# Mamba and mixture-of-experts layer on one core: shorter routing, the first two units' B spread by TensorE, and the slots of the schedule chosen anew

## What is computed

```python
xn = layernorm(x)
# branch 1 (Mamba): 512 channels, 16 states
x_in, z = split(xn @ W_in)
u = silu(causal_conv4(x_in) + conv_b)
dt, Bm, Cm = split(u @ W_xproj)
delta = softplus(dt @ W_dt + b_dt)
h[t] = exp(delta[t] * A) * h[t-1] + delta[t] * u[t] * Bm[t]      # per channel and state
y[t] = sum_n h[t][n] * Cm[t][n]
out1 = ((y + D_skip * u) * silu(z)) @ W_out
# branch 2 (experts): 16 experts, the best two of each row
probs = softmax(xn @ Wr + br); w, idx = top_k(probs, 2); w /= sum(w)
out2 = sum_k w[k] * (gelu(layernorm(xn @ W1[e] + b1[e])) @ W2[e] + b2[e]),  e = idx[k]
out = x + out1 + out2
```

## Time and profile before

| | |
|---|---|
| median of 3 runs | 1133.63 us (1129.92 to 1133.81) |
| profiled execution | 1137.55 us |
| its span, first to last instruction | 1135.8 us |
| mean granted TensorE clock | 0.902 |

### The profile page before, as it was taken

How to read it: one execution, slowest core, us unless ns; L and a number is a source line. 1 busy time by engine, 2 the same in 40 slices (tenths; PEclk the granted TensorE clock), 3 DMA queues, 4 the chain that set the end, 5 groups by cost and what they waited for, 6 DMA issues and landing times.

```text
span 1135.8 us, 16904 instructions
## 1 busy us (share of the span) xinstructions
PE 940.2 (83%) x4570; PEld 639.2 (56%) x4571; DVE 1045.8 (92%) x1308; ACT 864.9 (76%) x1839; POOL 871.0 (77%) x562
## 2 busy tenths in 40 slices
PE   4927776497998999779998999899988999887865
PEld 3414343363566656556666766576656666666544
DVE  7887999999999988968998989999999999999894
ACT  4544698556698799857999689978998799976971
POOL 5057899699778788756878767977987887887894
PEclk9957887589889999879997999899997999889989
DMA  9576457973376424825447652873457543855313
GB/s 305 188 271 241 137 183 225 316 291 83 112 245 204 107 69 122 312 82 112 103 104 233 210 107 67 255 235 57 107 151 249 133 116 87 291 169 108 70 19 65
DMA packets 119367, 185.86 MB, mean 164 GB/s; under 512 B 12012, under 2 KB 104344, under 8 KB 111016
## 3 DMA queue, kind: packets, MB, share of 16 engines
q1 hardware_dynamic: 87120, 144.60, 37.7%
q0 software_dynamic: 19584, 25.26, 13.0%
q10 hardware_dynamic: 12568, 14.93, 4.3%
HBM read 146.34 MB, written 42.60 MB: 166 GB/s over the span
## 4 chain that ended last, share of the span: by engine, by line
PE 36%; DVE 18%; issue 16%; ACT 14%; POOL 9%; DMA 4%; ACTq 2%; SPq 1%; POOLq 0%; DVEq 0%
DVE hb L1555 10%; PE psY L1087 8%; POOL hc L624 5%; PE psA L1112 4%; PE psC L1225 4%; PE psA L1160 3%; ACT hb L798 3%; PE psE L1202 3%; PE psC L1175 3%; PE psA L1104 2%; DVE psB L1544 2%; ACT hnT L913 2%; PE psA L1148 2%; DMA xg<-xs_d 1%; POOL xs_d L638 1%
## 5 line engine op out<-in xcount | busy, mean ns | idle before, releaser
L624 POOL TENSOR_TENSOR hc<-hb,Cb 128x1024 f32<-128x1024 f32 x245 | 621.2, 2640 | 108.2 <-PE psY L1087 65.4
L1555 DVE TENSOR_TENSOR_SCAN hb<-hb,carry,psB 128x512 f32<-128x512 f32 x384 | 470.9, 1261 | 6.8 <-ACT hb L798 5.0
L798 ACT ACTIVATE hb<-delta,aneg 128x512 f32<-128x512 f32 x512 | 351.9, 716 | 27.5 <-POOL hc L624 21.0
L1087 PE MATMUL psY<-ident,hc 128*128 128x128 f32 x2048 | 308.0, 292 | 71.1 <-POOL hc L624 70.8
L1087 PEld LDWEIGHTS psY<-ident,hc 128*128 128x128 f32 x2048 | 258.1, 151 | 183.8 <-POOL hc L624 94.1
L1544 DVE TENSOR_TENSOR psB<-Bb,psU 128x512 f32<-128x512 f32 x512 | 324.6, 678 | 3.2 <-DMA Bb<-bc_d 3.2
L672 POOL DMA_INDIRECT out<-yo,idx x80 | 128.8, 1610 | 56.8 <-DMA out<-yo,idx 16.9
L1555 DVE TENSOR_TENSOR_SCAN hb<-hb,psB 128x512 f32<-128x512 f32 x128 | 149.3, 1202 | 0.0
L1112 PE MATMUL psA<-ux,dgw 128*128 128x512 f32 x232 | 114.0, 607 | 1.6 <-ACT ux L739 1.4
L1225 PE MATMUL psC<-w2r,hnT 128*128 128x256 f32 x320 | 89.8, 429 | 0.0
L631 POOL TENSOR_TENSOR du<-delta,ux 128x512 f32<-128x512 f32 x32 | 47.2, 1474 | 53.9 <-DVE delta L1377 51.8
(11 more groups left out here) (233 smaller groups left out, 1198.2 us busy)
## 6 DMA issues: line engine op xcount, KB each, us to landing
Bb<-bc_d SPq DMA_DIRECT2D x32, 1024.0 KB, 7.1
Cb<-bc_d SPq DMA_DIRECT2D x32, 1024.0 KB, 7.4
w1r<-w1c_d SPq DMA_DIRECT2D x80, 256.0 KB
w2r<-in_L_ffn_W SPq DMA_DIRECT2D x80, 256.0 KB, 3.4
xg<-xs_d SPq DMA_DIRECT2D x20, 516.0 KB
xg<-xn_d SPq DMA_DIRECT2D x37, 128.0 KB, 2.8
Bb<-in_L_attn_x SPq DMA_DIRECT2D x8, 512.0 KB, 8.2
xn_d<-hb SPq DMA_DIRECT2D x8, 512.0 KB, 7.9
```

Source lines behind the costliest of these rows:

```text
L624: pool.tensor_tensor(hc[:, k:k + 2, :], hb[:, g % HR:g % HR + 2, :], Cb[:, n:n + 2, :], ALU.mult).then_inc(s_g, 1)
L798: act.activation(hb[:, g % HR, :], delta[:, dc, :], ACT.Exp, scale=aneg[:, dc, n:n + 1]).then_inc(s_exp, 1)
L1087: mm = pe.matmul(y[:, tt * P:(tt + 1) * P], hc[:, g % GR, tt * P:(tt + 1) * P], ident[:, :], start=False, stop=(n == NS - 1), is_transpose ...
L1555: dve.tensor_tensor_scan(h, h, psB[g % 2][:, :], first, ALU.mult, ALU.add).then_inc(s_scan, 1)
```

## The change

- *Norm tiles*: the last of the four tiles of each group is normalised by GpSimd (`norm_tile`), between its convolution weights. Readers wait for both counters; the statistics of a group wait until the tile two groups earlier is done.
- *Routing*: the one-hot selections run in two halves of 256 elements, each as soon as its half of the logits is copied. The second weight comes from exp(second logit - first), a 128 x 32 activation on ScalarE, and not from a masked sum. The rank matmul uses -1/0 weights (`later`) and a layout by experts, so that the copy, a subtraction, the comparison and its sum go; tiles per expert come from rounding count / 128. VectorE computes the slots ahead of the list of empty rows; GpSimd copies them to integers.
- *First units*: the rows of B of units 0 and 1 are spread by two TensorE matmuls (`b_all`) straight into the PSUM banks of the products; VectorE makes the first du, ScalarE copies it to PSUM behind the second exponential. SyncE loads the second quarter of B and C ahead of the rows. Eight of the 16 zero tiles are written in units 0 to 7 and not ahead of them.
- *Tables*: many slots of `AT`, `AT0`, `AT7` and `MOE` move; `HC_DVE` loses 204, 274 and 416 and gains 14 and 64; the additions of the last chunk come two slots earlier.

```diff
-INIT_AT = 58
-ETAB_AT = 40
+INIT_AT = 57
+ETAB_AT = 38
...
+BP = 2
...
 AT = {
-    "x_load": [36],
+    "x_load": [34],
...
-    "xd_mm": [39, 41, 41, 44],
+    "xd_mm": [41, 41, 42, 43],
...
-    "d_max": [55, 58, 62, 4],
-    "du": [53, 0, 25, 26],
+    "d_max": [55, 59, 63, 5],
+    "du": [53, 0, 23, 26],
...
 AT0 = {
...
-    "d_mm": [46, 50, 59, 6],
...
-    "d0_exp": [4, 6, 6],
-    "d0_max": [7, 8, 8],
-    "du": [50, 8, 21, 35],
...
+    "d_mm": [49, 51, 60, 1],
...
+    "d0_exp": [3, 6, 7],
+    "d0_max": [3, 4, 7],
+    "du": [50, 7, 20, 32],
...
 AT7 = {
...
-    "p_tr": [53, 56, 59, 61],
-    "p_trc": [56, 58, 59, 62],
-    "p_mm": [56, 58, 59, 61],
-    "p_copy": [58, 58, 61, 62],
+    "p_tr": [48, 56, 57, 58],
+    "p_trc": [56, 57, 58, 59],
+    "p_mm": [56, 57, 59, 60],
+    "p_copy": [57, 58, 59, 60],
 }
 
-HC_DVE = [2, 10, 12, 20, 54, 56, 86, 180, 204, 274, 416]
+HC_DVE = [2, 10, 12, 14, 20, 54, 56, 64, 86, 180]
...
+ZERO0 = 8
+ZERO_STEP = 1
...
 MOE = {
-    "load": [0],
-    "load1": [0, 3],
-    "load2": [12],
+    "load": [1],
+    "load1": [1, 3],
+    "load2": [13],
...
-    "idx": [6],
+    "idx": [4],
...
+def zero_unit(k):
+
+    return (k - ZERO0) * ZERO_STEP
...
+        def norm_tile(eng, g, tt):
+
+            eng.wait_ge(s_rs, g + 1)
...
             load_bc(0, 0)
+            load_bc(0, 1)
             sp.wait_ge(s_w["bst"], 16 * 6)
             sp.wait_ge(s_route, 1)
             for j in range(NPLACE):
                 load_rows(j)
-            for q in range(1, NS // NQ):
+            for q in range(2, NS // NQ):
                 load_bc(0, q)
...
             pool.wait_ge(s_w["conv"], 32)
-            for dc in range(DC):
-                conv_weights(dc)
+            for g in range(NC):
+                norm_tile(pool, g, TT - 1)
+                if g >= 1 and g - 1 < 2 * DC - 2:
+                    conv_weights((g - 1) // 2, (g - 1) % 2)
+            for h in range(2):
+                conv_weights(DC - 1, h)
...
-            du_mul(0, 0)
+
+            pool.wait_ge(s_slots, 1)
+            pool.tensor_copy(slots[:, :, :], small[:, 5:7, :]).then_inc(s_route, 1)
             for k in range(NPAD):
-                put_zeros(k)
+                if zero_unit(k) < 0:
+                    put_zeros(k)
...
+                if g == 1:
+                    act.wait_ge(s_du0, 1)
+                    act.activation(psU[:, :], du[:, :], ACT.Copy).then_inc(s_dup, 1)
...
-            act.wait_ge(s_rtd, 1)
+            act.wait_ge(s_rtd, 3)
             act.activation(scratch[7], scratch[6], ACT.Exp).then_inc(s_rte, 1)
+            act.wait_ge(s_rtd, 5)
+            act.activation(small[:, 6, :], small[:, 7, :], ACT.Exp).then_inc(s_rte, 1)
...
+            def b_all(n):
+
+                if n == 0:
+                    pe.wait_ge(s_slots, 1)
...
+                bank = psB[n] if n < 2 else psY[1]
+                pe.matmul(bank[:, :], ident[0:NS, n:n + 1].to_broadcast([NS, P]), xr[0:NS, :], start=True, stop=True).then_inc(s_b0, 1)
...
-            for dc in range(3):
+            d_mm(0, 0)
+            for n in range(2):
+                b_all(n)
+            for dc in range(1, 3):
                 d_mm(0, dc)
...
-                for tt in range(TT):
-                    dve.tensor_scalar(xnb[g][:, tt, :], xraw[g][:, tt, :], mv[:, g % 2, tt, 0:1],
-                                      rstd[:, g % 2, tt:tt + 1], ALU.subtract, ALU.mult).then_inc(s_xn, 1)
+                for tt in range(TT - 1):
+                    norm_tile(dve, g, tt)
...
+            for h in range(2):
+                part = slice(h * T // 2, (h + 1) * T // 2)
+                half = slice(h * TILES // 2, (h + 1) * TILES // 2)
+                dve.wait_ge(s_lg, h + 1)
+                top = onehot(h, lg, s32(0), s32(1), oh1, row[0], row[1])
...
+                onehot(h, row[4], s32(2), s32(3), oh2, row[0], row[1])
...
             dve.wait_ge(s_rank, 2)
-            link(dve.tensor_copy(ei(row[3]), psB[1][:, :].rearrange("p (i e) -> p e i", e=E)))
-            link(dve.tensor_tensor_scan(row[4], reset, row[3], 0.0, ALU.mult, ALU.add))
-            link(dve.tensor_tensor(row[6], row[4], row[3], ALU.subtract))
+            link(dve.tensor_tensor_scan(row[4], reset, psB[1][:, :], 0.0, ALU.mult, ALU.add))
             count = ei(row[4])[:, :, TILES - 1]
-            link(dve.tensor_tensor(ei(row[7]), count.unsqueeze(2).to_broadcast([P, E, TILES]), ei(iotaJ), ALU.is_gt))
-            link(dve.tensor_reduce(s16(8), ei(row[7]), AX.X, ALU.add))
...
             d_max(0, 0)
...
+            dve.wait_ge(s_delta, 1)
+            dve.tensor_tensor(du[:, :], delta[:, 0, :], u_of(0, 0), ALU.mult).then_inc(s_du0, 1)
...
+                if g < 2:
+                    dve.wait_ge(s_b0, g + 1)
+                    dve.tensor_tensor(psB[g][:, :], psB[g][:, :], du[:, :], ALU.mult).then_inc(s_dbu, 1)
+                    return
```

## The result

The changed kernel takes 1124.52 us (median of 7 runs, 1119.69 to 1129.40), the kernel before 1131.86 us beside it (1129.15 to 1133.81): a ratio of 0.9937, with a 95% interval of 0.9913 to 0.9961. The profiled execution of the changed kernel is 1126.54 us long, its span 1124.8. One of the six runs of experiment 12 took 1362.62 us and stands outside its ratio.

The account below looks back on a forecast made before the run. VectorE, busy for 92% of the span, was taken as the clock. Terms -13.2 -3.1 +1.2 -9.0 -3.0 -3.0 = -30.1 from the profiled 1137.55 us gave 1107.4, less 2.4: 1105; the 8-in-10 range was 1094 to 1121.

Parts of the forecast that it names:

- 204, 274 and 416: Units whose products with C leave VectorE: gains of 9.0, 3.0 and 3.1 us from waits and work taken away.
- Up to the first product: Opening until VectorE's first product with B: it starts at 62.4 us, 6.5 us before 68.91; bounds 4.5 to 8.
- the routing chain: VectorE's opening chain to delta's maximum: done at 59.5 us, ahead of TensorE's and ScalarE's chain at 61.0, which decides.
- The tile's term: Opening: one of four normalising tiles per group goes to GpSimd, taking 2.6 us off VectorE over eight groups.
- Behind it: Opening behind the first product: earlier products with C on GpSimd and fewer waits, net 6.7 us.
- check by stations: Counting VectorE's work from the first product at 62.4 us: scan of units 16 and 17 at 103.6, against 116.8 before.
- rival 2: Behind the first hundred units, where DMA queues are full: 10 of the opening's 13.2 us come back, 1115 us; chance 0.08.
- rival 1: Waits at 204 and 274 are TensorE's lateness, paid back at next gates; only opening, 416, 64, end count: 1118 us; chance 0.18.
- VectorE then goes on until it lacks exponentials: Behind unit 204: VectorE runs until unit 213's exponential, scan ending at 522.9 us instead of 531.9, a gain of 9.0 us.
- The argument against: Against waits at 204 and 274 being paid back at later gates: TensorE has 17% of idle time to catch up.
- Slots moved within 6 us either way, taken at nothing: Moved slots of AT, AT7 and MOE: no change within even-odd pairs, others taken at nothing, bounds 6 us either way.
- End: Last chunk's addition into the output issued ahead of the last pair: 3.0 us, other chain delayed by 0.8 only; bounds 0 to 3.

Follow-up runs that it names:

- experiment 12: Changed kernel with the initial copy of x at unit 72, last pair's product with C on VectorE, experts' group 5 begun at 196: 1122.07 us, ratio 0.9923.
- second pair of profiles: One more profiled execution of each kernel, both unchanged: kernel before 1126.06 us, changed kernel 1120.49 us.
- experiment 4: Changed code with all unit tables, product list, copy's unit and experts' table's unit of the kernel before: 1124.04 us, ratio 0.9954.
- experiment 5: Kernel before, old opening kept, with the changed kernel's unit tables, product list, copy's unit and experts' table's unit: 1134.03 us, ratio 1.0037.
- experiment 1: Changed kernel with the products with C of units 204, 274 and 416 given back to VectorE: 1120.89 us, ratio 0.9926.
- experiment 6: Changed kernel with the initial copy at unit 72, old units of chunks 1 to 7 and experts, 204, 274, 416 on VectorE: 1115.61 us, ratio 0.9886.
- experiment 7: Changed kernel with half the contraction left out of some TensorE products of units 197 to 222, output not the reference's: 1115.54 us, ratio 0.9860.
- experiment 10: Both kernels again unchanged (before profiled 1126.06, changed 1125.03 us median); changed kernel with last chunk's transposes and output products at their old units: 1123.14 us, ratio 0.9940.
- experiment 11: Changed kernel with last pair's product on VectorE: 1121.96 us; also copy at 72, last chunk two units earlier: 1116.66; last two pairs, one unit earlier: 1115.55.

## Why the prediction was wrong, by its own steps

In the prediction's own terms 30.1 us were forecast and 5.6 found (second pair of profiles). Of the 24.5 us between them 3.9 are missing by unit 88 (8.1 us instead of 13.2 less 1.2), 17.1 between there and the last scan (15.1 forecast, 2.0 lost) and 3.5 in the tail. The largest step that failed is the one for 204, 274 and 416.

- **Up to the first product**: right in size (6.0 and 5.3 us against 6.5). VectorE came to the maximum of delta without a wait, at 61.43 us, and ScalarE's logarithm had ended at 61.05 (60.42 plus 0.63): the routing chain decided by 0.4 us, where the other was forecast to decide by 1.5. TensorE's and ScalarE's chain came as forecast (61.05 against 61.0), VectorE's 1.9 us late (61.43 against 59.5), and it used up the slack. The tile's term was 0.8 to 1.1 us, not 2.6; two writes of Mb (L1544) took 0.91 us each from start to next start instead of 0.46.
- **Behind it**: 6.7 us forecast, 4.3 us by unit 16 (106.5 us where the check by stations said 103.6). Of the 2.9 us by which that scan is late, 0.5 are the first product's and 2.5 are VectorE's product of unit 10, which took 3.71 us instead of 1.2 (timeline of the changed kernel):

```profile
88.99 3.71 DVE L1646 TENSOR_TENSOR hc<-hb,Cb 128x1024 f32<-128x1024 f32 x1
89.26 2.35 POOL L657 TENSOR_TENSOR hc<-hb,Cb 128x1024 f32<-128x1024 f32 x1
```

  The forecast had priced this meeting of VectorE and GpSimd at 416 and allowed for it at 64, and not in the opening, where it moved GpSimd's products. It took 2.00 to 3.83 us in the thirteen profiles with the new opening and the new units of chunk 0, and 1.23 us with either of them alone.
- **The opening's gain kept** (rival 2, 0.08): 14.2 us at unit 56 became 8.1 at unit 88. Rival 2 named the place and the transfers, and was answered with the argument that they are issued by unit number. They are; but the rows' transfers behind the copy then take as long as they take, and ScalarE's order turned one late row buffer into a late delta. As it stands rival 2 is wrong too: the opening alone loses only 0.5 us there (experiment 4), and the new units lose more with the old opening (experiment 5). What was lost is what the new units of chunk 0 had won.
- **204, 274 and 416** (15.1 us): worth nothing that the medians show (experiments 1 and 6; these bound it by about 5 us). This is rival 1 (0.18) for 204 and 274, and this was the larger error; rival 1 still counted 416, and that came back too. The evidence was at hand: TensorE 39.19 of 40 us busy. The step that failed was "VectorE then goes on until it lacks exponentials": it followed VectorE to the exponential of unit 213 and stopped there, with a gain of 9 us, instead of asking when the gate of 224 could be ready. Counted from unit 200 that gate began after 55.1 and 53.6 us in the two profiles of the kernel before and after 53.6 and 52.7 us in the changed kernel, 1.0 to 1.5 us sooner where 9.0 were forecast; VectorE waited 1.0 us for it before and 7.3 us after the change. (With 204 given back in experiments 1 and 6 it is 56.7 us, so 3 to 4 us of the term stand at that gate, and they too are gone at the end of experiment 6.) What filled the stretch is TensorE's work at least in part: with 10 us less of it 4 to 5 us came through (experiment 7). The argument against, 17% of idle TensorE time, is an average over the span.
- **Slots moved within 6 us either way, taken at nothing**: for chunks 1 to 7 right (0.3 us with the rest, experiment 6). For chunk 0 wrong twice: its units gave 6.5 us by unit 56, and its third delta, whose maximum and activations now share slot 63, cost 5 to 8 us at unit 64 (ledger, first and second pair). The prediction looked at the maxima, which moved within an even-odd pair, and not at the activations ahead of them, which moved from 59 to 63.
- **End** (3.0 us): 0. "The other chain is delayed by 0.8 only" was wrong: the addition on GpSimd holds the last pair by its wait and its issue, and the last gate's wait grew by 3.8 us. Where GpSimd kept up, 1.4 to 2.6 us of the term came (experiment 10).
- **The base.** The sum was made against 1137.55 us and 2.4 us taken off. The medians of the sessions were 1129.7 to 1131.9, so 3 to 5 us more were due. That is in my favour and hides as much of the error: taken from these medians, the terms would have given 1100 to 1102 us.

Rival 1's 1118 us and the 6 us lost between units 56 and 88 give 1124, the time measured, but in part by luck: rival 1 still counted 416 (3.1 us) and the end (3.0 us), which didn't come, and stands on a base (1137.55 less 1.5) that was 4 to 6 us above the medians. The range took the rivals one at a time, and two that rest on different stretches add up.

## What to carry to other kernels

A wait taken from one engine is worth something only if the next station at which that engine needs the others comes earlier too: follow the other engines' chain to the next gate, and count the gain there, not where the wait was. A stretch where two engines are full can be tested by giving one of them less work, and not by moving work within it. When a table of slots moves a step, look at the distance between the step and its reader, and at what each engine's own order has behind an instruction that waits for a transfer: here a step three units ahead of its reader cost nothing, and in the reader's own slot, behind such a wait, 5 to 8 us. When an edit has two halves, run each half alone before naming the one that is to blame. And run a second profile before pricing a wait of 1 or 2 us.

## What the runs showed of the hardware

- VectorE's product of two SBUF operands, when it meets GpSimd's, ends 1.09 us behind it: 92.70 against 91.61 us in the changed kernel, and 101.92 against 100.83 in experiment 11, where 1.22 us of work took 4.45. In both its start stands ahead of GpSimd's, by 0.27 and 0.46 us, and it is held all the same; at 96.17 us in the changed kernel, 1.01 us ahead, it ran through in 1.28 us. The Trainium skill (SBUF — State Buffer, section "SBUF: two separate sides") has an exclusive lock on a shared pair of ports, and that the one which starts first gets it. That one is held until the other is done agrees with these rows; that the first start wins doesn't, by the starts that the profile gives. The normalising tiles, one tensor and two scalars per row, weren't held: three of VectorE's took 1.10 us at 19.41 us, beside GpSimd's of 19.09 to 20.37, and 1.03 us at 16.74, where GpSimd's tile was done and it made convolution weights.
- A normalising tile of 128x256 takes 1.22 to 1.52 us on GpSimd and 0.34 to 0.41 on VectorE, a factor of about 3.5. The Trainium skill (GPSIMD Engine Reference, section "Engine selection") has one-input operations on GpSimd at roughly line rate; these rows differ, and the rows decide. The product of 128x1024 takes 2.36 to 2.95 and 1.22 us, a factor of about 2.
- The two profiles of the kernel before differ by 11.5 us in span without one disturbed stretch: in each of six places one lost 1.3 to 3.5 us.
